# Thirty-six extra products of the identity on TensorE behind each turnover of a graph-attention kernel

## The reference

```
def gatv2_layer(x, Ws, bs, Wd, bd, attn, src, dst):
    hs = (x @ Ws + bs).reshape(N, H, HD)
    hd = (x @ Wd + bd).reshape(N, H, HD)
    hs_e = hs[src]
    e = jax.nn.leaky_relu(hs_e + hd[dst], SLOPE)
    logits = jnp.einsum('ehd,hd->eh', e, attn)
    m = jax.ops.segment_max(logits, dst, num_segments=N)
    ex = jnp.exp(logits - m[dst])
    s = jax.ops.segment_sum(ex, dst, num_segments=N)
    alpha = ex / s[dst]
    out = jax.ops.segment_sum(alpha[..., None] * hs_e, dst, num_segments=N)
    return jax.nn.elu(out).reshape(N, DM)
h = x
for l in range(L):
    h_new = gatv2_layer(h, Wsrc[l], bsrc[l], Wdst[l], bdst[l], attn[l], src, dst)
    h = layer_norm(h_new + h, ln_w[l], ln_b[l])
```

## Time and profile before

| | us |
|---|---|
| median of 3 runs | 2263.32 (2262.71 to 2266.45) |
| the profiled execution | 2268.95 |
| its span, first to last instruction | 2267.2 |
| TensorE busy | 2145.1 (95%) |
| VectorE busy | 1700.6 (75%) |
| ScalarE busy | 1127.1 (50%) |
| GpSimd busy | 863.9 (38%) |

### The profile page before, as it was taken

How to read it: one execution, slowest core, us unless ns; L and a number is a source line. 1 busy time by engine, 2 the same in 40 slices (tenths; PEclk the granted TensorE clock), 3 DMA queues, 4 the chain that set the end, 5 groups by cost and what they waited for, 6 DMA issues and landing times. The chain is left out here.

```text
span 2267.2 us, 86951 instructions
## 1 busy us (share of the span) xinstructions
PE 2145.1 (95%) x31067; PEld 1707.9 (75%) x31067; DVE 1700.6 (75%) x4454; ACT 1127.1 (50%) x2759; POOL 863.9 (38%) x847
## 2 busy tenths in 40 slices
PE   8999999998999999999997999899999999999788
PEld 4665555555888888888887656688988888888676
DVE  5325995354888888888887764488988888888884
ACT  1101200024666666666664324466666666666584
POOL 0000002012555556556552311355565565565121
PEclk9999999999999999999998999999999999999889
DMA  5001035144788788788784124478888888777411
GB/s 191 1 1 66 21 111 139 69 123 128 231 252 251 236 254 247 239 254 247 244 249 145 49 94 123 139 242 246 251 249 246 251 244 253 243 242 240 171 45 48
DMA packets 141035, 401.11 MB, mean 177 GB/s; under 512 B 21753, under 2 KB 79388, under 8 KB 140708
## 3 DMA queue, kind: packets, MB, share of 16 engines
q0 software_dynamic: 59584, 298.64, 42.8%
q1 hardware_dynamic: 78109, 90.41, 12.8%
q10 hardware_dynamic: 3044, 7.45, 1.0%
HBM read 368.18 MB, written 16.78 MB: 170 GB/s over the span
## 5 line engine op out<-in xcount | busy, mean ns | idle before, releaser
L497 ACT ACTIVATE at_relu<-at_turned,ah_attn_size 128x512 f32<-128x512 f32 x1092 | 721.2, 694 | 457.9 <-PE at_turned L556 453.2
L478 POOL DMA_INDIRECT at_rows<-table,ah_index x360 | 389.6, 1082 | 276.9 <-DVE ah_index L690 170.3
L478 POOL DMA_INDIRECT ah_room<-table,ah_index x352 | 381.4, 1084 | 284.2 <-DVE ah_index L690 193.4
L554 PE MATMUL at_turned<-ah_place,dst_rows 96*128 96x128 bf16 x2208 | 403.6, 223 | 26.3 <-issue 26.2
L556 PE MATMUL at_turned<-ident,ah_room 128*128 128x128 f32 x2208 | 419.9, 280 | 3.4 <-issue 3.4
L556 PE MATMUL at_turned<-ident,at_rows 128*128 128x128 f32 x2160 | 405.0, 277 | 3.7 <-issue 3.6
L554 PE MATMUL at_turned<-at_place,dst_rows 96*128 96x128 bf16 x2160 | 390.1, 222 | 6.1 <-issue 6.1
L680 DVE SCALAR_TENSOR_TENSOR sums<-sums,at_factor,at_total 128x97 f32 x1456 | 344.8, 309 | 23.4 <-PE at_total L592 6.8
L556 PEld LDWEIGHTS at_turned<-ident,ah_room 128*128 128x128 f32 x2208 | 318.8, 144 | 31.0 <-issue 7.1
L556 PEld LDWEIGHTS at_turned<-ident,at_rows 128*128 128x128 f32 x2160 | 308.5, 143 | 25.0 <-issue 3.3
L670 DVE TENSOR_TENSOR at_spread<-at_lined,at_weight 128x1024 f32<-128x1024 f32 x182 | 223.7, 1229 | 98.6 <-ACT at_weight L507 91.6
(11 more groups left out here) (311 smaller groups left out, 3236.0 us busy)
## 6 DMA issues: line engine op xcount, KB each, us to landing
at_flags<-run_flags SPq DMA_DIRECT2D x182, 64.0 KB
dst_rows<-pr_parts SPq DMA_DIRECT2D x76, 144.0 KB, 2.5
ah_place<-local_rows SPq DMA_DIRECT2D x92, 96.0 KB
at_place<-local_rows SPq DMA_DIRECT2D x90, 96.0 KB
table<-ah_room SPq DMA_DIRECT2D x20, 400.0 KB, 2.4
ah_room<-table,ah_index POOLq DMA_INDIRECT x368
at_rows<-table,ah_index POOLq DMA_INDIRECT x360
mx_w<-in_L_mix_W_qkv SPq DMA_DIRECT2D x4, 1152.0 KB, 11.8
```

Source lines behind the costliest of these rows:

```text
L478: pool.indirect_dma_start(rows[b][:, j, :], None, table, bass.IndirectOffsetOnAxis(index[b][:, j:j + 1], 0)).then_inc(gathered[b], 16)
L497: act.activation(relu[c][:], turned[chunk(b, c)][:], ACT.Relu, scale=attn_size[:, c:c + 1]).then_inc(bent, 1)
L554: pe.matmul(into, dst_rows[:, bass.ds(at[j], 1), c * P:(c + 1) * P].rearrange("p o d -> p (o d)"), place[b][:, j * P:(j + 1) * P], start=T ...
```

## The change

Behind the last destination product, in both turnovers, TensorE issues 36 matmuls with the identity as both operands. Their results go to the eight 128-column slices of the PSUM tile `turned`, which nobody reads any more. They wait for nothing and signal nothing. Nothing else is changed.

```
--- before.py
+++ after.py
@@ -1551,6 +1551,9 @@
 assert sum(n for _, n in TURN_PARTS) == NT
 
 
+WARM = 36
+
+
 def turned_in(turn):
 
     return range(TURN_PARTS[turn][0], sum(TURN_PARTS[turn])) if 0 <= turn < TURNS else ()
@@ -1793,6 +1796,8 @@
                     if settle and t + 1 < NT:
                         turn_tile(NT + t + 1)
                     product(NT + t, w_dst)
+                for n in range(WARM):
+                    pe.matmul(turned[:, n % 8 * P:(n % 8 + 1) * P], ident[:], ident[:], start=True, stop=True)
 
             @block.vector
             def _(dve):
```

## The result

The changed kernel takes 2271.07 us, median of 11 runs (2267.56 to 2276.33), beside 2263.32 us for the kernel before in 11 runs (2256.97 to 2267.60). The ratio is 1.0036, with an interval of 1.0025 to 1.0047: slower by 7.75 us, outside the predicted range. The profiled execution took 2270.84 us, close to its median; its span is 2269.1 us and the mean clock 0.984.

What follows compares the result with a forecast made beforehand. TensorE is busy in nearly every slice, but at the turnovers SyncE's barrier and VectorE's copy end last. Products 0, earlier pairs 0 and one clock fall +1.5 on 2263.32 gave 2264.8 us, range 2262.0 to 2267.8.

Steps and rivals of the forecast that it cites:

- What bounds the places: At both turnovers: SyncE arrives last at the barrier; behind it TensorE needs VectorE's `at_linear` copy, at 557.87 and 1454.30.
- Part one, the products themselves: Before each barrier: the 36 products take 8.31 us, hidden by SyncE's wait for stores; cost 0, at most 1.3 us.
- I take 0: Products before the barriers: SyncE's store wait hides them with 0.1 to 0.2 us to spare, so they add nothing.
- the sum: Whole kernel: products 0, earlier pairs 0, one clock fall +1.5, added to the median 2263.32, giving 2264.8 us.
- the rivals: Both turnovers: no fall 0.22, two short falls 0.18, one or both long 0.10, faster 0.05, barrier later 0.04, no effect 0.03.
- Part two, the clock: Start of each attend: twenty pairs at full clock, 4.5 us less TensorE work together, none of it on the path.
- Part three, the new fall: Idle 2.4 and 2.35 us before line 563; a clock fall six in ten per turnover, costing 1.5 us each.
- The rule in the Trainium skill: Pairs at attend's start: transposes don't count as busy for the clock, so a fall is all but certain, sum +3.0.

Runs made afterwards that it cites:

- e7_tiny: Kernel before plus 36 one-column products at the place of the change in each turnover: ratio 1.0029, 2273.79 beside 2265.79 us.
- e16_align: Changed kernel plus two groups of 28 one-column products, restoring the edge loops' places in blocks of 256 instructions: 0.9999 against the kernel before, 2263.62 us.
- e4_after: The changed kernel as it is, timed again beside the kernel before: ratio 0.9996, 2762.99 beside 2763.15 us.
- e11_align: Changed kernel plus two groups of 28 one-column products, restoring places in blocks of 256 instructions: ratio 0.9998 against the kernel before, 2761.12 us.

## Why the prediction was wrong

**What bounds the places: right.** SyncE sets the barrier, 8.5 us behind the last product, and VectorE's copy releases line 563, 7.3 us behind the barrier, as predicted.

**Part one, the products themselves: right in place, wrong in price.** Predicted 72 records in 8.2 to 8.4 us; measured 8.20. The barrier is still SyncE's, its release 8.5 us behind the last product, with 0.3 to 0.4 us to spare.

The step that failed stands in this part: "I take 0", with an upper bound of 1.3 us, because nobody waits for `turned` "and no other engine has an instruction more". It priced the 144 instructions per turnover by the time they take where they stand. `e7_tiny` measures what they cost the whole program with neither the warmth nor the new idle time: +6.6 us (3.9 to 9.5). That this price arises in the written-out list behind them, by its moved blocks, is what `e16_align` speaks for with its 0.9999; how the moved blocks cost the time stays open, as the table above shows. The row for it was in hand, the 1.66 us of "issue" in the earlier trace rows; I used it as an idle time that the clock survived and didn't ask what the wait was for, nor what would move it. The same omission is in the sentence of the sum that "the terms do not depend on where the other time lies", and none of the rivals had this mechanism, so that the range had no room for it.

**Part two, the clock: right.** First pairs at 1.00 (553.80 to 557.10) and the last of the twenty begins near 556.7, 3.3 us behind the first, as worked out. The gain went where it was sent, into waiting for `at_linear`: 2.51 and 2.52 us, predicted 2.4 and 2.35. Release to line 563 is unchanged. That the copy, once early, would have let the 4.5 us through isn't shown; under the other condition it didn't.

**Part three, the new fall: right.** One fall in the two turnovers of the profiled execution, at 0.50 for 3.3 us, so +1.5 us as priced. The first message products of layer 0 (line 592), in the kernel before and in the changed one:

```profile
565.12 1.58 PE L592 MATMUL at_total<-ah_room,at_spread 128*32 128x100 f32 x64
```
```profile
568.35 1.58 PE L592 MATMUL at_total<-ah_room,at_spread 128*32 128x100 f32 x64
```

They start 565.12 - 550.6 = 14.5 and 568.35 - 552.2 = 16.1 us behind the release of the barrier, 1.6 us later with the change; in layer 1, where the clock didn't fall, the two agree to 0.1 us. Which of the two layers has a fall was left to chance in the prediction. The rule in the Trainium skill, "TensorE: Matmul & The Clock Gate", section "Part 4: PE-mode transpose", would have let both fall; here one did, and the clock stayed at 1.00 through 3.3 us of pairs of which half are transposes, so this trace bears it out only in part.

**The sum again.** With the missing term: +6.6 for the added instructions as `e7_tiny` has them, and +1.5 for the fall of the clock, together 8.1 us, beside a measured 7.75 (0.36% is 8.1). That they agree so closely is luck, since the first term is known only to within 3.9 to 9.5. And the change with its blocks put back, `e16_align`, comes out at -0.2 us with an interval of -4.3 to +3.9, which holds the +1.5 of the forecast but can't tell it from 0.

## What to carry to other kernels

An instruction that waits for nothing and that nobody waits for can still have a price if a long written-out list stands behind it: here 36 one-column products in each of two places cost 0.29%. The likely reason is that they move the places at which that engine waits for its instructions. Before such an edit, look for idle times that the profile gives to no one, see whether they recur at a fixed count of instructions, and test the edit against a twin that adds as many tiny instructions, and against one filled up to the next whole block, and, which is missing here, against one filled up to no whole block. Where a change of a few us is judged in a kernel of thousands of instructions, without such twins its own effect and that of the shift can't be told apart.

## What the runs showed of the hardware

**Waits at a fixed place behind a multiple of 256 instructions.** In a list without loops TensorE loses 23 to 34 us of 1287 to waits of up to 2.5 us that no other engine ends. All those over 0.3 us in the edge loops stand 24 to 27 instructions behind a multiple of 256, and only some of the places that come shortly behind small matmuls have one (27 to 43 of some 110 in the four traces). I hadn't expected it to be 2 to 3% of those stretches, in a kernel whose TensorE is "95% busy".

**Two speeds of the edge loop.** The same kernel took 2263 to 2266 us beside three of the nineteen kernels timed, and 2732 to 2765 us beside the sixteen others, `e4_after` among them. One chip showed both: `e11_align` (2761.12) and `e16_align` (2263.62) are the same kernel on the same chip. The stages outside the two attends took 892 to 897 us either way. A hundred microseconds inside the loop of layer 0, first the kernel before as in the first profile, then `e0_before`, the same kernel (columns as in the earlier trace rows):

```profile
800.00:900.00 100.00, 98.20 (x2046) 88.36 (x2045) 88.63 (x261) 65.70 (x177) 59.29 (x55) 1.00 0.82 250
```
```profile
800.00:900.00 100.00, 81.96 (x1477) 68.20 (x1478) 65.67 (x190) 50.12 (x131) 40.06 (x40) 0.98 0.59 181
```

and TensorE's longest wait in `e0_before`, 700 to 800 us, in total, times, longest:

```profile
PE at_total L592 <- issue: 16.5, 26, 1.2
```

A macro tile takes 10.2 us instead of 7.2, GpSimd gathers 40 times instead of 55, the DMA moves 181 GB/s instead of 250, and TensorE has waits inside line 592 that the first profile doesn't have. GpSimd isn't busier and each gather isn't longer (948 ns against about 1040), so neither engine is seen to be the cause. What sets the speed stays open. It fits with it that most ratios here are 1.000: TensorE is busy for 82% of that time, and waits at the places behind a multiple of 256 no longer stand out. That the one is the reason for the other wasn't tested.

**The clock falls after short idle times.** In the changed kernel an idle time of 1.78 us was followed by 0.50 at once, one of 2.51 us after 2.1 us, and one of 2.52 us not at all (1454.00 to 1460.00 at 1.00). In `e16_align` one of 2.07 us at the barrier of layer 1 was followed by 0.50 from 1446.2 to 1449.5, where the change has 1.6 us and keeps its clock, and its 2.53 us in the loop were followed by 0.50 at once. The length of the idle time alone doesn't tell.
